# Stationary operands of 128 columns in the value projection and the score matmuls of a gated cross-attention kernel

## The chip, the cores and the metric

The kernel runs on one core of one Trainium2 chip. The metric is the device time of one execution in microseconds; the median of three runs of the kernel before is 411.07 us (410.23 to 413.1).

## The reference, cut to what matters

A block of gated cross-attention is followed by a gated mixture of experts. There are 8 sequences of 56 tokens with 256 features, and each has a context of 1500 rows with 256 features. Only the attention is touched by the change.

```python
q = _qdq(x) @ _qdq(wq).T + bq                       # (8, 56, 256), int8 fake quantisation
kv = cond @ wkv.T + bkv                             # cond: (8, 1500, 256)
k, v = jnp.split(kv, 2, axis=-1)                    # 16 heads of 16 features each
attn = jax.nn.softmax(jnp.einsum('bnhd,bmhd->bhnm', q, k) * scale, axis=-1)
o = jnp.einsum('bhnm,bmhd->bnhd', attn, v).reshape(B, N, C)
out = _qdq(o) @ _qdq(wp).T + bp
```

After it come the residual, a layer norm, the choice of two of 16 experts for every token, the experts (silu gates, at most 128 tokens each) and the sum.

## The kernel before, in words

The program is one block with one instruction stream for each engine, written out by hand, and semaphores between them. Three parts follow each other in time: the first projections of sequence 0 with the quantisation of the queries, then 64 attention slots, then the output projection and the experts.

A slot `u` is one pair of heads of one sequence: `b, i = divmod(u, 8)`. In slot `u` TensorE runs (function `pe_slot`)

- `scores(u)`: three matmuls of 500 context rows each. The stationary operand is the pair's part of `QC`, 112 columns (2 heads x 56 tokens) by 96 rows; the moving operand is the stacked keys `KS`. VectorE takes the row maxima from them (line 794).
- a projection for the next sequence (`project`, line 1035 through the helper `split3`). K0 to K5 are the keys: two feature halves by three chunks of 500 context rows, 6 matmuls with 500 moving columns, the stationary operand being 128 columns of the weights `wkvT`. V0 to V5 are the values: two tiles of 125 context rows each, 12 matmuls with 256 moving columns (the weights), the stationary operand being 125 columns of the context `cT`. Each value is a sum of three half-precision products (`SPLIT`), hence six matmuls for a tile.
- `turn_maxima(u - 1)`: one small matmul (line 1088) that turns the maxima into two rows of a PSUM bank. Its stationary operand is two columns wide and goes to the last quarter of the array's columns (`tile_position=(0, QR)`).
- a second projection or the attention outputs of two pairs (line 1112), in turn.
- `turned_scores(u - 1)`: 12 matmuls with 112 moving columns that compute the scores once more, turned, with the maxima subtracted (line 1101). Their stationary operand is `KS`, 128 columns since long, ScalarE takes the exponential of the result (line 501).

Which projection stands in which slot is a table:

```python
order = ("K0", "K1"), ("K2",), ("K3", "V0"), ("K4",), ("K5", "V1"), ("V2",), ("V3", "V4"), ("V5",)
```

The first name of a slot runs right behind `scores`, the second right behind `turn_maxima`. So V2, V3 and V5 follow the score matmuls, and V0, V1 and V4 follow the small matmul of line 1088. This holds for the 7 sequences 1 to 7; sequence 0 is projected before the slots, in an order of its own.

The context of a sequence is loaded in three chunks of 500 rows. ScalarE makes the upper halves (line 479), and the lower halves come from VectorE for sequences 0 and 1 (line 715) and from GpSimd from sequence 2 on (line 395). `need_lo(pe, n, c)` lets TensorE wait for chunk `c` of sequence `n`. `cT` and `QC` hold two sequences each.

GpSimd makes `QC` in two halves for each sequence (function `queries`, line 419, semaphore `qc_done`); `scores` waits for half 0 in slot `i = 0` and for half 1 in slot `i = 4`. At its start GpSimd fills constants (line 365 and those behind it); TensorE and VectorE wait until the count `EARLY` of them is reached.

Of the kernel before, what the change touches and what calls it, by code (L numbers as in the profile page):

```python
# [41 lines left out]
EPS = 1e-5  # L42
EARLY = 16
NCONST = 24
NSMALL = 3 * 16
# [64 lines left out]
def program(nc, x, ctx, cols, rows, gate, wq, wkv, wp, W13, W2, out):  # L110
    stack = ExitStack()
    with stack:
        def sb(name, shape, dt=F32):
            return stack.enter_context(nc.sbuf_tensor(name, shape, dt))
# [48 lines left out]
        q16 = sb("q16", [QR, NPAIR, T], F16)  # L163
        QC = sb("QC", [128, 2, QW], F16)
        par16 = sb("par16", [128, 2], F16)
        wkvT = sb("wkvT", [128, 2, NH, 2 * D], F16)

        c_in = sb("c_in", [128, NH, M])
        cT = sb("cT", [128, 2, 2, NH, M], F16)

# [87 lines left out]
        def need(eng, name, n):  # L258

            if n > 0:  # L260
                eng.wait_ge(s[name], n)
# [100 lines left out]
        def _(gp):  # L362
            c = Steps(gp, s["consts"])
            for t, v in ((mhalf, -0.5), (unmagic, -MAGIC), (ident, 0.0), (ident16, 0.0), (ones, 1.0), (ones16, 1.0), (before16, 1.0), (hm2, 1.0)):
                c.did(gp.memset(t[:], v))
# [662 lines left out]
        def _(pe):  # L1028
# [30 lines left out]
            def project_values(n, v):  # L1059
                bank = take(("V", n, v))  # L1060
                need_lo(pe, n, v // 2)
                for k in range(2):
                    t = 2 * v + k
                    last = split3(PS[0:KP, bank, k * D:(k + 1) * D], lambda a, h: cT[:, n % 2, a, h, t * KP:(t + 1) * KP],
                                  lambda a, h: wkvT[:, a, h, D:2 * D])
                last.then_inc(s["v_ready"], 1)

            def scores(u):
                b, i = divmod(u, NPAIR)
                need(pe, "aug_done", min(u - 1, SLOTS - NPAIR))  # L1070
                if i % 4 == 0:
                    need(pe, "qc_done", 2 * b + i // 4 + 1)
                for c in range(CH):
                    if i % 4 == 0:
                        pe.wait_ge(stacked[i // 4][c], 48 * (b + 1))
                    if c < 2:
                        need(pe, "red_done", 2 * (u - 1) + c + 1)
                    mm(PS[0:TP, c, 0:CW], QC[0:QR, b % 2, i * TP:(i + 1) * TP], KS[0:QR, b % 2, i, c * CW:(c + 1) * CW],  # L1078
                       start=True, stop=True).then_inc(s["sc_ready"], 1)
# [357 lines left out]
```

## Time and profile before

| | us |
|---|---|
| median of the three runs | 411.07 |
| lowest and highest run | 410.23, 413.1 |
| span of the profiled execution, first to last instruction | 405.0 |
| median less the span (what lies around it) | 6.07 |
| TensorE matmuls busy in the span | 358.6 |
| TensorE weight loads busy in the span | 269.3 |
| VectorE busy | 303.5 |
| ScalarE busy | 250.9 |
| GpSimd busy | 124.1 |

The profile is one execution. Times are read from the start of the span. PE is TensorE's matmul side and PEld its weight loads, which lie beside matmuls; the end of a matmul in the profile is modelled, so from one matmul to the next the starts are to be compared, not the ends. A row such as "64.23 1.47 ... x12" says that 12 instructions of one kind began at 64.23 us and that 1.47 us lie between the first start and the last end. DVE is VectorE, ACT ScalarE, POOL GpSimd, SP the queue that issues most transfers.

### The profile page before, as it was taken

Reading aid. Unit: us, or ns where it says so; the run is one execution under the profiler, and the core shown is the slowest. Engines: PE = TensorE matmul, PEld = TensorE weight load, DVE = VectorE, ACT = ScalarE, POOL = GpSimd, SP = SyncE. Lnnn points to the kernel's source line nnn. Section 1 sums busy time; section 2 is a strip of 40 time slices with the busy share of each in tenths; the row PEclk is TensorE's granted clock in tenths of the full one; section 3 lists DMA queues with packets and bytes.
Section 4 is the critical chain, followed back from the end, with each engine's and each line's share of the span. In section 5 each row is a group of like instructions: output and inputs, shape, how many; then the busy total and the mean of one; then the engine's idle time right before and its main releaser. Section 6 shows DMA issues by size and latency. Waiting matters only on the chain.

```text
span 405.0 us, 14019 instructions
## 1 busy us (share of the span) xinstructions
PE 358.6 (89%) x5793; PEld 269.3 (67%) x5793; DVE 303.5 (75%) x656; ACT 250.9 (62%) x412; POOL 124.1 (31%) x116
## 2 busy tenths in 40 slices
PE   0896899999998998998999999998864699999993
PEld 0663468668677766855866776786643587888882
DVE  3888886775776676586577668668896877999993
ACT  3476477777686676776768666567721535666761
POOL 6151462132022122222203300001101054787870
PEclk9999699999999999999999999999985858999998
DMA  7869965565294186166336208544000009635001
GB/s 253 196 157 197 241 146 134 87 159 136 58 171 115 53 152 182 54 106 175 103 61 125 54 14 142 129 137 141 3 2 2 1 1 306 191 116 163 2 0 45
DMA packets 34512, 45.65 MB, mean 113 GB/s; under 512 B 3995, under 2 KB 30299, under 8 KB 34323
## 3 DMA queue, kind: packets, MB, share of 16 engines
q1 hardware_dynamic: 33395, 43.74, 44.5%
q0 software_dynamic: 640, 0.78, 0.9%
q8 instruction: 46, 0.75, 0.8%
q10 hardware_dynamic: 416, 0.26, 0.3%
q14 instruction: 15, 0.12, 0.1%
HBM read 25.08 MB, written 0.47 MB: 63 GB/s over the span
## 4 chain that ended last, share of the span: by engine, by line
PE 76%; DVE 13%; issue 5%; ACT 2%; POOL 2%; DMA 1%; DVEq 0%; ACTq 0%; POOLq 0%
PE PS L1035 35%; PE PS L1101 9%; PE PS L1078 8%; PE PS L1112 7%; PE PS L1363 4%; PE PS L1322 3%; DVE mx L794 2%; PE PS L1088 2%; PE PS L1346 2%; PE PS L1312 1%; DMA x_in<-x 1%; DVE KN L743 1%; PE PS L1279 1%; DVE st L697 1%; DVE mtop L798 1%
## 5 line engine op out<-in xcount | busy, mean ns | idle before, releaser
L794 DVE TENSOR_REDUCE mx<-PS 112x1 f32<-112x500 f32 (+1 forms) x128 | 114.3, 933 | 52.8 <-PE PS L1078 52.7
L501 ACT ACTIVATE PT_all<-PS 128x1344 f32<-128x1344 f32 x64 | 82.6, 1290 | 10.1 <-PE PS L1101 9.9
L1035 PE MATMUL PS<-cT,wkvT 128*128 128x500 f16 x288 | 71.5, 385 | 18.0 <-POOL slot_of L404 11.2
L1035 PE MATMUL PS<-wkvT,cT 128*125 128x256 f16 x576 | 73.2, 279 | 0.0
L1035 PEld LDWEIGHTS PS<-wkvT,cT 128*125 128x125 f16 x576 | 65.3, 139 | 5.3 <-issue 0.5
L395 POOL TENSOR_TENSOR cT<-c_in,cT 128x1000 f16<-128x1000 f32 x18 | 37.5, 2082 | 86.9 <-ACT cT L479 86.9
L1035 PEld LDWEIGHTS PS<-cT,wkvT 128*128 128x128 f16 x288 | 27.5, 99 | 50.8 <-POOL slot_of L404 11.2
L486 ACT ACTIVATE KN<-PS,col_in 128x500 f16<-128x500 f32 x48 | 32.5, 677 | 40.6 <-PE PS L1035 40.6
L1078 PE MATMUL PS<-arena,QC 96*112 96x500 f16 x192 | 52.4, 380 | 3.1 <-issue 2.8
L1101 PE MATMUL PS<-QC,arena 98*128 98x112 f16 x768 | 49.2, 214 | 3.0 <-ACT QC L521 2.9
L493 ACT ACTIVATE V<-PS 125x512 f32<-125x512 f32 x48 | 28.7, 598 | 30.6 <-PE PS L1035 30.6
L1101 PEld LDWEIGHTS PS<-QC,arena 98*128 98x128 f16 x768 | 41.6, 99 | 8.3 <-ACT QC L521 3.1
L743 DVE SCALAR_TENSOR_TENSOR KN<-PS,col_in,KN 128x500 f16<-128x500 f32 x48 | 35.2, 736 | 12.8 <-ACT KN L486 12.0
L1112 PE MATMUL PS<-PT_all,V 125*17 125x56 f32 x2592 | 37.8, 213 | 0.1
L449 POOL TENSOR_TENSOR arena<-arena 88x512 f16<-88x512 f32 x17 | 24.8, 1458 | 31.2 <-ACT arena L527 31.1
L1035 PE MATMUL PS<-arena 88*128 88x256 f16 (+2 forms) x216 | 33.3, 306 | 0.8 <-ACT arena L635 0.7
L1112 PEld LDWEIGHTS PS<-PT_all,V 125*17 125x17 f32 x2592 | 33.3, 98 | 0.2 <-issue 0.2
L419 POOL TENSOR_TENSOR QC<-q,par 96x448 f16<-96x448 f16 x16 | 15.0, 943 | 57.1 <-PE PS L1101 55.3
L1035 PEld LDWEIGHTS PS<-arena 88*128 88x128 f16 (+2 forms) x216 | 22.5, 106 | 9.0 <-issue 1.2
L1078 PEld LDWEIGHTS PS<-arena,QC 96*112 96x112 f16 x192 | 20.3, 132 | 9.8 <-issue 3.8
L479 ACT ACTIVATE cT<-c_in 128x1000 f16<-128x1000 f32 x24 | 24.9, 1036 | 2.0 <-DMA c_in<-ctx 1.6
L1088 PEld LDWEIGHTS PS<-ident,nm 112*2 112x2 f16 x64 | 5.1, 79 | 21.9 <-issue 17.3
(207 smaller groups left out, 463.8 us busy)
## 6 DMA issues: line engine op xcount, KB each, us to landing
arena<-KN SPq DMA_DIRECT2D x144, 125.0 KB, 3.6
c_in<-ctx SPq DMA_DIRECT2D x24, 500.0 KB, 4.5
cT<-W SPq DMA_DIRECT2D x11, 352.0 KB
c_in<-W SPq DMA_DIRECT2D x6, 352.0 KB
cT<-W SPq DMA_DIRECT2D x11, 176.0 KB
arena<-place_far SPq DMA_DIRECT2D x1, 1568.0 KB, 10.0
c_in<-W SPq DMA_DIRECT2D x6, 176.0 KB
PT_all<-L_xattn_wkv SPq DMA_DIRECT2D x1, 512.0 KB, 6.1
```

The costliest lines, as they stand in the source:

```text
L395: gp.tensor_tensor(cT[:, n % 2, 1, :, c * CW:(c + 1) * CW], c_in[:, :, c * CW:(c + 1) * CW], cT[:, n % 2, 0, :, c * CW:(c + 1) * CW], ALU. ...
L449: gp.tensor_tensor(w2T[j % 2][:, 1], w2_s, w2T[j % 2][:, 0], ALU.subtract).then_inc(s["w2l_done"], 1)
L479: act.activation(cT[:, n % 2, 0, :, c * CW:(c + 1) * CW], c_in[:, :, c * CW:(c + 1) * CW], ACT.Copy).then_inc(s["th_done"], 1)
L486: act.activation(KN[:, oh, c, 0, :], PS[:, BANK["K", n, u], 0:CW], ACT.Identity, bias=bk_c[:, oh:oh + 1]).then_inc(s["kh_done"], 1)
L493: act.activation(V[:, n % 2, 2 * v:2 * v + 2, :, 0:DH], PS[0:KP, BANK["V", n, v], :].rearrange("p (t h j) -> p t h j", t=2, h=H), ACT.Copy ...
L501: act.activation(PT_all[:, u % 4, :].rearrange("p (c k) -> p c k", c=CH), PS[:, 3:6, 0:4 * TP], ACT.Exp, scale=SCORE).then_inc(s["exp_done ...
L743: dve.scalar_tensor_tensor(KN[:, oh, c, 1, :], PS[:, BANK["K", n, u], 0:CW], bk_c[:, oh:oh + 1], KN[:, oh, c, 0, :], ALU.add, ALU.subtract ...
L794: dve.tensor_reduce(mx[:, u % 2, k:k + 1], PS[0:TP, k:1 + k * (CH - 1), 0:CW], AX.XY, ALU.max).then_inc(s["red_done"], 1)
L1035: ins = mm(out_, w(a, h), x_(b, h), start=first and k == 0, stop=last and k == len(todo) - 1)
L1078: mm(PS[0:TP, c, 0:CW], QC[0:QR, b % 2, i * TP:(i + 1) * TP], KS[0:QR, b % 2, i, c * CW:(c + 1) * CW], start=True, stop=True).then_inc(s[" ...
L1101: last = mm(PS[:, 3 + t // 4, (t % 4) * TP:(t % 4 + 1) * TP], KS[0:QR + 2, b % 2, i, t * KP:t * KP + 128], QC[0:QR + 2, b % 2, i * TP:(i + ...
L1112: last = mm(PS[32 * j:32 * j + VW, bank, 0:S], V[:, b % 2, t, 4 * hg + j, :], PT[:, (2 * g + j // 2) % 4, t * TP + (j % 2) * S:t * TP + (j ...
```

## The change

The value projection's stationary operand gets 128 columns of `cT` instead of 125: the further three are the first rows of the next tile. They give three further rows of the result, which nobody reads. The context's last tile reads columns 1500 to 1503, so `cT` gets 1504 columns, and GpSimd fills the last four with zeros at its start. Where a tile now reaches into the next chunk (V1 and V3), the wait is for that chunk; in sequence 0 those two tiles (t = 3 and 7) stay at 125 columns. The score matmuls get 128 columns of `QC` instead of 112: the further 16 belong to the next pair, or for the last pair to 16 columns behind the end, which are filled with zeros. The wait for the second half of `QC` therefore moves from slot `i = 4` to slot `i = 3`. The two fills are counted among GpSimd's constants.

```diff
-EARLY = 16
-NCONST = 24
+EARLY = 18
+NCONST = 26
...
-        QC = sb("QC", [128, 2, QW], F16)
+        QC = sb("QC", [128, 2, QW + 128 - TP], F16)
...
-        cT = sb("cT", [128, 2, 2, NH, M], F16)
+        cT = sb("cT", [128, 2, 2, NH, KW], F16)
...
             c = Steps(gp, s["consts"])
+            c.did(gp.memset(cT[:, :, :, :, M:KW], 0.0))
+            c.did(gp.memset(QC[:, :, QW:], 0.0))
...
             def project_values(n, v):
                 bank = take(("V", n, v))
-                need_lo(pe, n, v // 2)
+                over = n > 0 and v % 2 == 1 and v < 5
+                need_lo(pe, n, v // 2 + over)
                 for k in range(2):
                     t = 2 * v + k
-                    last = split3(PS[0:KP, bank, k * D:(k + 1) * D], lambda a, h: cT[:, n % 2, a, h, t * KP:(t + 1) * KP],
+                    w = KP if n == 0 and t in (3, 7) else 128
+                    last = split3(PS[0:w, bank, k * D:(k + 1) * D], lambda a, h: cT[:, n % 2, a, h, t * KP:t * KP + w],
                                   lambda a, h: wkvT[:, a, h, D:2 * D])
...
-                if i % 4 == 0:
-                    need(pe, "qc_done", 2 * b + i // 4 + 1)
+                if i in (0, 3):
+                    need(pe, "qc_done", 2 * b + (i + 1) // 4 + 1)
...
-                    mm(PS[0:TP, c, 0:CW], QC[0:QR, b % 2, i * TP:(i + 1) * TP], KS[0:QR, b % 2, i, c * CW:(c + 1) * CW],
+                    mm(PS[:, c, 0:CW], QC[0:QR, b % 2, i * TP:i * TP + 128], KS[0:QR, b % 2, i, c * CW:(c + 1) * CW],
```

The order of TensorE's matmuls stays as it was. What moves is one wait. On TensorE, sequence 0, these are the score matmuls of slots 3 and 4 before the change, with what each waits for:

```order
L1078 MATMUL PS<-arena,QC 112x500 [waits red_done,aug_done]
L1078 MATMUL PS<-arena,QC 112x500 [waits red_done]
...
L1078 MATMUL PS<-arena,QC 112x500 [waits stacked1_0,red_done,qc_done,aug_done]
L1078 MATMUL PS<-arena,QC 112x500 [waits red_done,stacked1_1]
```

and the same place with the change:

```order
L1082 MATMUL PS<-arena,QC 128x500 [waits red_done,qc_done,aug_done]
L1082 MATMUL PS<-arena,QC 128x500 [waits red_done]
...
L1082 MATMUL PS<-arena,QC 128x500 [waits red_done,stacked1_0,aug_done]
L1082 MATMUL PS<-arena,QC 128x500 [waits red_done,stacked1_1]
```

The wait for the second half of the queries stands one slot earlier; `arena` is the memory of the stacked keys.

## Rows read from the trace of the kernel before

**Rows 1.** The page: busy time of the engines, and the chain that ended last

```profile
PE 358.6 (89%) x5793; PEld 269.3 (67%) x5793; DVE 303.5 (75%) x656; ACT 250.9 (62%) x412; POOL 124.1 (31%) x116
PE 76%; DVE 13%; issue 5%; ACT 2%; POOL 2%; DMA 1%; DVEq 0%; ACTq 0%; POOLq 0%
```

**Rows 2.** Busy time of each engine in stretches: the steady slots, and around 44 us

```profile
core 0: us, PE busy (x) PEld busy (x) DVE busy (x) ACT busy (x) POOL busy (x), PEclk, DMA share, GB/s
56.00:272.00 216.00, 209.97 (x4043) 156.13 (x4043) 149.16 (x308) 150.07 (x225) 45.92 (x29) 1.00 0.51 113
...
40.80:48.00 7.20, 6.20 (x26) 2.94 (x27) 5.29 (x9) 3.27 (x4) 2.11 (x4) 0.53 1.09 254
```

**Rows 3.** Groups of instructions, shapes apart: projections and scores, matmuls and weight loads

```profile
L1035 PE MATMUL PS<-wkvT,cT 128*125 128x256 f16 x576 | 73.2, 279 | 0.0
L1035 PEld LDWEIGHTS PS<-wkvT,cT 128*125 128x125 f16 x576 | 65.3, 139 | 5.3 <-issue 0.5
L1035 PEld LDWEIGHTS PS<-cT,wkvT 128*128 128x128 f16 x288 | 27.5, 99 | 50.8 <-POOL slot_of L404 11.2 <-issue 7.6 <-DVE cT L715 2.8
L1078 PEld LDWEIGHTS PS<-arena,QC 96*112 96x112 f16 x192 | 20.3, 132 | 9.8 <-issue 3.8 <-DVE mx L794 0.5 <-ACT sp_row L558 0.4
```

**Rows 4.** Timeline of TensorE's matmuls, value slots: V3 and V4 between scores

```profile
63.59 0.80 PE L1078 MATMUL PS<-arena,QC 96*112 96x500 f16 x3
64.23 1.47 PE L1035 MATMUL PS<-wkvT,cT 128*125 128x256 f16 x12
65.64 0.21 PE L1088 MATMUL PS<-ident,nm 112*2 112x112 f16 x1
65.78 1.52 PE L1035 MATMUL PS<-wkvT,cT 128*125 128x256 f16 x12
67.14 0.76 PE L1101 MATMUL PS<-QC,arena 98*128 98x112 f16 x12
67.73 0.80 PE L1078 MATMUL PS<-arena,QC 96*112 96x500 f16 x3
```

**Rows 5.** The same stretch on the side of the weight loads

```profile
64.02 1.44 PEld L1035 LDWEIGHTS PS<-wkvT,cT 128*125 128x125 f16 x12
...
65.77 1.28 PEld L1035 LDWEIGHTS PS<-wkvT,cT 128*125 128x125 f16 x12
...
67.68 0.39 PEld L1078 LDWEIGHTS PS<-arena,QC 96*112 96x112 f16 x3
```

**Rows 6.** Timeline of TensorE's matmuls, a key slot: K0 and K1 around line 1088

```profile
105.26 1.43 PE L1035 MATMUL PS<-cT,wkvT 128*128 128x500 f16 x6
106.62 0.21 PE L1088 MATMUL PS<-ident,nm 112*2 112x112 f16 x1
106.76 1.44 PE L1035 MATMUL PS<-cT,wkvT 128*128 128x500 f16 x6
```

**Rows 7.** Timeline of TensorE's matmuls, two places where scores start after a wait

```profile
255.20 0.84 PE L1078 MATMUL PS<-arena,QC 96*112 96x500 f16 x3 [0.66 <-issue]
...
274.38 0.84 PE L1078 MATMUL PS<-arena,QC 96*112 96x500 f16 x3 [0.22 <-ACT sp_row L558]
```

**Rows 8.** Timeline of all engines at the start: GpSimd's fills and TensorE's first matmul

```profile
0.84 0.10 POOL L365 MEMSET unmagic<- 112x1 f32 x1
...
7.16 1.04 POOL L390 TENSOR_TENSOR rstd<-var,mhalf 112x4 f32<-112x4 f32 x1 [1.84 <-DVE var L703]
...
11.20 2.66 PE L1035 MATMUL PS<-cT,wkvT 128*128 128x500 f16 x6 [11.20 <-POOL slot_of L404]
```

**Rows 9.** Timeline of GpSimd, the second half of QC for sequences 0 and 1

```profile
29.59 0.92 POOL L419 TENSOR_TENSOR QC<-q,par 96x448 f16<-96x448 f16 x1 [0.97 <-DMA q<-PT_all]
...
51.10 1.82 POOL L419 TENSOR_TENSOR QC<-q,par 96x448 f16<-96x448 f16 x2
```

**Rows 10.** Timeline of TensorE's matmuls around 44 us

```profile
40.84 2.50 PE L1035 MATMUL PS<-cT,wkvT 128*128 128x500 f16 x6 [2.35 <-DVE cT L715]
...
45.56 1.46 PE L1078 MATMUL PS<-arena,QC 96*112 96x500 f16 x3
```

## The prediction

> **What bounds the kernel now.** I read four views, from the coarse to the fine. The page's engines and its chain come first [rows 1]: TensorE's matmuls are busy for 358.6 us of 405.0, and 76% of the chain that ended last is TensorE. The reader is to see that a nanosecond taken from TensorE is likely to be a nanosecond of the whole, but that busy time alone does not say which of its instructions cost anything, since the weight loads (PEld, 269.3 us) lie beside the matmuls. Then the table by stretches [rows 2]: from 56 to 272 us, the steady slots, matmuls are busy for 209.97 of 216.00 us at a granted clock of 1.00, which is the level of 2.4 GHz. All other engines are under 151 us there. So in the slots TensorE goes from one matmul to the next without a pause, and what matters is the distance from start to start. Then the groups with shapes apart [rows 3]: a weight load of 125 columns is recorded at 139 ns, one of 112 columns at 132 ns, and one of 128 columns at 99 ns, although it loads more. That is the difference the change reaches for: 576 loads of the first kind and 192 of the second become loads of the third. Last the timeline of two value slots [rows 4, 5] and of a key slot [rows 6], which tell whether a load is waited for at all.
>
> **What a weight load costs where it lies.** In the stretch of V3, which follows the score matmuls, the first load begins at 64.02 us [rows 5] and the first matmul that uses it at 64.23 [rows 4]: the load lies beside the last score matmul. The twelve matmuls take 1.47 us to the end of the last, whose recorded length is about 0.28 [rows 3], so the distance is (1.47 - 0.28) / 11 = 0.108 us. The keys, whose loads are all of the short kind, give the rate of the array itself. Three scores start 64.23 - 63.59 = 0.64 us ahead of the next run, 0.21 each, and 0.80 - 2 x 0.21 = 0.38 us is the recorded length of a matmul of 500 columns [rows 4]. So six keys lie (1.43 - 0.38) / 5 = 0.21 us apart for 500 moving columns [rows 6], which is 0.1075 us for 256. The values thus run at the rate of their moving columns already; a load of 125 columns hides behind every matmul of 256. I price the loads inside a run of values at nothing. Their cover is the matmul before, 0.108 us long, and it stays.
>
> The load of the first score matmul has a shorter cover. It begins at 67.68 us [rows 5], and the matmul at 67.73 [rows 4]; before it stand the matmuls of line 1101, at a distance of (0.76 - 0.21) / 11 = 0.05 us. 67.14 + 12 x 0.05 = 67.74, so the scores start right on time: nothing to gain there either. The second and third score load lie behind 0.21 us each.
>
> What is left are the loads with no cover. The small matmul of line 1088 uses a quarter of the array's columns of its own, and the next load begins only behind it: at 65.77 us, when its matmul begins at 65.78 [rows 4, 5]. The run of values behind it takes 1.52 us instead of 1.47, so 0.05 us are paid for the bare load of 125 columns. The keys tell what is paid for a bare load of 128: K1 behind line 1088 takes 1.44 us, K0 behind the scores 1.43, so 0.01 us [rows 6]. The change saves 0.04 us at each such place.
>
> **The Trainium skill on this.** The groups show the 128-column load shorter than the 125-column one, 99 against 139 ns [rows 3]. The Trainium skill, page "TensorE: Matmul & The Clock Gate", section "Weight-path perf modes — Fast Weight Load (FWL) and DoubleRow", says why: the fast load comes on by itself where the stationary operand has 128 columns and is not single precision, and it was measured about twice as fast. The trace agrees in kind, with 99 against 139 ns recorded. The same page, section "Back-to-back issue gap", says that in a stream of loads and matmuls the distance is set by both together; that rule speaks for more than I forecast, and it is the second rival below. By it the sum would be some 29 us, by the rows on the starts it is about 1.
>
> **The sum.** V0, V1 and V4 of seven sequences follow line 1088: 3 x 7 = 21 places x 0.04 = 0.84 us. Two score groups start after a wait and are 0.84 us long instead of 0.80 [rows 7]: 2 x 0.03 = 0.06 us at best. The values of sequence 0 run ahead of the slots between other work; I give them nothing. The remaining edits:
> - Two more fills on GpSimd ahead of its constants. The nearest rows are its fills of 0.10 us [rows 8]; a strided one may take twice that, so 0.2 to 0.4 us. GpSimd then waits 1.84 us for VectorE before the power at 7.16 us, and TensorE's first matmul is at 11.20 [rows 8]; the wait hides both fills. Without that cover they would cost 0.4 us at most.
> - The wait for the second half of `QC` one slot earlier, in slot 3. Behind it on TensorE stand the scores and the whole slot, for which VectorE and ScalarE wait. For sequence 0 that half is done at 29.59 + 0.92 = 30.5 us [rows 9]; the scores of slot 2 start at 45.56 [rows 10], those of slot 3 behind them. For sequence 1 it is done at 51.10 + 1.82 = 52.9 us [rows 9], and its slot 3 comes eight slots later than that of sequence 0. Price: nothing.
> - The wait of V1 and V3 for the next chunk. K1 and K2 of the same sequence, two to six slots earlier on the same engine, already waited for chunks 1 and 2. Nothing.
> - Three or sixteen further rows of results: the matmul's time goes by its moving columns; the keys write 128 rows at the same rate as the scores write 112 [rows 4, 6]. Nothing.
>
> Bounds of the whole: at the bare places from 0 to the full 0.05 us (0 to 1.05); inside the runs (0.108 - 0.1075) x 555 is 0.3 us at best, and as much lost if rounding goes the other way. So -1.4 to +0.3 us. I take 0.84 + 0.06 = 0.9, from the row of K1. All of it lies on the path, since TensorE runs without a pause there. The profiled execution then goes from a span of 405.0 to 404.1; 6.07 us lie around the span to the median of 411.07, and I count them as unchanged: 410.2 us. The three runs lie between 410.23 and 413.1, so a median may differ by about 1 us of itself.
>
> **Rivals.**
> 1. The first load stays bare at its old price, because the short load needs something that tiles at odd offsets of 125 columns do not have, or the 0.04 us come back as a longer wait. For it: the short loads in the trace are of `wkvT` and the stacked keys, none of `cT` or `QC`. Against it: the stacked keys are read at offsets of 125 columns too and load in 99 ns on line 1101. Time: 411.1 us.
> 2. The recorded load time is all on the path: 576 x (139 - 99) = 23.0 us and 192 x (132 - 99) = 6.3 us, 29.4 us in all [rows 3], so 411.07 - 29.4 = 381.7 us. For it: PEld is busy for two thirds of the span. Against it: 139 ns of load do not fit one behind the other into a distance of 108 ns, so they overlap. The Trainium skill's rule on the distance, named above, is this rival's.
> 3. Slower: TensorE's clock falls once more. At 40.8 to 48.0 us the granted clock is 0.53, the level of 1.2 GHz for nearly all of it, behind a wait of 2.35 us for VectorE [rows 2, 10], and six key matmuls take 2.50 us instead of 1.43. The price of one such stretch is 6.20 x (1 - 0.53) = 2.9 us of busy time. If TensorE, done sooner, waits longer in the pauses of the slots and the clock falls there too, the time is 410.2 + 2.9 = 413.1 us. It decides from one more such fall on, as one costs three times the gain. Against it: the clock is 1.00 over all of 56 to 272 us, pauses included, and 0.04 us make no pause.
>
> **How the numbers follow.** Forecast 80%: 410.2 us, of itself 409.3 to 411.5. Rival 1 9%: 411.1. Rival 2 4%: 381.7. Rival 3 7%: 413.1. The range from 408.8 to 412.6 holds the forecast with its bounds, the spread of medians and rival 1; it leaves out rivals 2 and 3, and with a little of the forecast's own tail that is under 2 in 10. A change of 1% (4.1 us) is about what a measurement of this kernel can tell from none. Faster by more than that is rival 2 and little else: 5%. Slower by more needs rival 3 with a second fall: 3%. Within 1%: 92%.
>
> **What would show it.** In the profile after, the value and score loads should read about 99 ns in the groups and PEld's busy time should fall by some 29 us, while matmuls keep their distance of 0.108 and 0.21 us. The run of values behind line 1088 should take 1.48 us instead of 1.52, the one behind the scores still 1.47. The slots from 56 to 272 us should shorten by some 0.8 us. I am wrong if a run of values behind the scores gets shorter as well, if scores start sooner than 0.05 us behind line 1101, if a pause that is not there now stands in front of slot 3, or if the granted clock falls below 1.00 in the slots.

## The result and the profile after

The changed kernel takes 407.63 us (median, 404.54 to 409.92), the kernel before, run beside it, 410.15 us (406.56 to 413.78). The ratio is 0.9947, with a 95% interval of 0.9923 to 0.9971: 0.5% faster, some 2.2 us. The ratios in this document leave out executions more than 1.5% above the fastest of the same kernel, while the times are medians of all, among them single executions of 523.54 us (before_later_sum), 604.38 us (after_shift128) and 1925.24 us (after_shift64_later_sum). The forecast of 410.2 us meant 0.9 us less than before, and its range ended at 408.8. So the direction and a change within 1% came as forecast, the time fell out of the range, and more than half of the gain came from somewhere else. Of the 2.6 us between forecast and result, 0.9 are the base: I counted from 411.07, the median of three runs; the median of twenty is 410.15.

The profiled execution of the changed kernel has a span of 406.1 us and took 407.8 us. Its page, with the engines, the queue that carries instructions, and the chain:

```profile
PE 357.6 (88%) x5793; PEld 255.5 (63%) x5793; DVE 304.8 (75%) x656; ACT 250.8 (62%) x412; POOL 124.8 (31%) x118
...
q8 instruction: 47, 0.77, 0.9%
...
PE 78%; DVE 13%; issue 4%; ACT 2%; DMA 1%; POOL 1%; DVEq 0%; ACTq 0%; POOLq 0%
```

Weight loads are busy for 13.8 us less than in [rows 1], TensorE's matmuls for 1.0 us less. The span is 1.1 us longer than that of before, though the kernel is faster: single executions of either kernel scatter by some 3 us either way, and the profiled one of before was among its quickest (two more executions, below, have spans of 409.6 and 409.9). That also corrects the table ahead: 1.7 us lie around the span, not 6.07.

Groups with shapes apart, weight loads (busy, mean ns of one, idle before):

```profile
L1037 PEld LDWEIGHTS PS<-wkvT,cT 128*128 128x128 f16 x564 | 54.2, 99 | 14.2 <-issue 1.7
...
L1037 PEld LDWEIGHTS PS<-cT,wkvT 128*128 128x128 f16 x288 | 27.7, 99 | 54.4 <-issue 12.2 <-POOL zero L404 11.2 <-DVE cT L717 2.9
L1082 PEld LDWEIGHTS PS<-arena,QC 96*128 96x128 f16 x192 | 15.6, 98 | 10.0 <-issue 1.7 <-DVE mx L796 0.6 <-ACT sp_row L560 0.4
```

Lines have moved by two to four: 1035 is now 1037, 1078 is 1082, 1088 is 1092, 1101 is 1105, 1112 is 1116. Against [rows 3] the loads of the values went from 139 to 99 ns, those of the scores from 132 to 98. The change does what it says.

The timeline of TensorE's matmuls in the slot of V3 and V4:

```profile
66.82 0.80 PE L1082 MATMUL PS<-arena,QC 96*128 96x500 f16 x3
67.46 1.47 PE L1037 MATMUL PS<-wkvT,cT 128*128 128x256 f16 x12
68.86 0.21 PE L1092 MATMUL PS<-ident,nm 112*2 112x112 f16 x1
69.00 1.48 PE L1037 MATMUL PS<-wkvT,cT 128*128 128x256 f16 x12
70.33 0.76 PE L1105 MATMUL PS<-QC,arena 98*128 98x112 f16 x12
70.92 0.80 PE L1082 MATMUL PS<-arena,QC 96*128 96x500 f16 x3
```

The reader sees the forecast come true to the hundredth: the values behind the scores take 1.47 us as before, those behind line 1092 take 1.48 instead of 1.52 [rows 4], scores start 0.59 us behind the start of line 1105's run as they did. Score start to score start, the slot takes 4.10 us instead of 4.14.

**Where the other gain is.** I cut both executions at the starts of the score groups. From slot 6 to 12, six slots, the kernel before takes 24.05 us and the changed one 23.97, and each of the next sequences repeats that (24.04 and 23.97 from slot 14 to 20, 22 to 28, 30 to 36). But the slots left out between them (12 and 13, 20 and 21, 28 and 29, 36 and 37, 44 and 45, 51 to 53) differ by more: 59.36 us in all before, 57.77 after. One of them in the kernel before, slot 36, on TensorE's timeline:

```profile
185.47 1.39 PE L1112 MATMUL PS<-PT_all,V 125*17 125x56 f32 x96
186.79 0.76 PE L1101 MATMUL PS<-QC,arena 98*128 98x112 f16 x12
187.39 0.80 PE L1078 MATMUL PS<-arena,QC 96*112 96x500 f16 x3
189.83 1.44 PE L1035 MATMUL PS<-cT,wkvT 128*128 128x500 f16 x6 [1.63 <-POOL cT L395]
```

and the same slot of the changed kernel:

```profile
188.48 1.39 PE L1116 MATMUL PS<-PT_all,V 125*17 125x56 f32 x96
189.80 0.77 PE L1105 MATMUL PS<-QC,arena 98*128 98x112 f16 x12
190.40 0.80 PE L1082 MATMUL PS<-arena,QC 96*128 96x500 f16 x3
191.04 0.58 PE L1037 MATMUL PS<-cT,wkvT 128*128 128x500 f16 x2
192.20 1.00 PE L1037 MATMUL PS<-cT,wkvT 128*128 128x500 f16 x4 [0.58 <-issue]
```

TensorE stands still in both. Before, it does so for 1.63 us between the scores and the keys; the profile names GpSimd's write of `cT`, though the same chunk had been waited for slots earlier. After, it is for 0.58 us, in the middle of six matmuls of one accumulation, where no wait can stand; the profile says "issue". Such a pause stands once in every sequence, and in the trace of before its places are exactly 618 matmuls apart (behind matmul 953, 1571, 2189, 2807, 3425; the sixth, behind 4044, is 619 on), after the change mostly 619.

What comes every 618 matmuls? In the changed kernel TensorE has 5793 matmuls, as many loads and, counted in the trace, 434 instructions that only wait: 12,020. One of two queues that carry instructions (q8 in the page above) moved 0.77 MB in 47 packets, 16 KB each; 12,020 / 47 is 255.7, so 256 instructions a packet. And in the kernel before, 618 matmuls with their loads and 44 waits are 1,280 instructions, five packets. So I read it as follows: TensorE's instructions come in blocks of 256, and at the end of one in five it stands still until the next has come. That block's last instructions lie behind the 96 small matmuls of the attention outputs (line 1112), which with their loads use up 192 instructions in 1.39 us, three quarters of a block; the rest of such a slot, 22 matmuls, takes some 2.7 us, 16 instructions per us. In slots 12 to 44 of every trace without a shift the packet's transfer starts 2.2 to 2.9 us before TensorE goes on, however long the pause. The counts say the same for all runs: the traces but that of after_shift128 hold 86 pauses over 0.25 us in slots 6 to 54, and in each the number of TensorE's instructions (matmuls, loads and waits) ahead of the pause leaves 192 or 193 when divided by 256. None lies more than 28 matmuls behind the outputs; four lie among them.

A sequence is 620 matmuls, 1,284 instructions with its 44 waits: four more than five blocks, so the pause moves two matmuls towards the outputs in each sequence. The kernel before has 442 waits, the changed one 434, one less in a sequence. In the traces a load holds one wait itself and a wait instruction one or two more. In slots 3 and 4 the first score matmuls had two and four waits (the order shown with the change), which took one and two wait instructions; now they have three each, which take one and one. So its pauses come 618 or 619 matmuls apart and stand elsewhere: in the six sequences 0, 1, 2, 2, 3 and 3 matmuls further behind the outputs than before. At 0.21 us a matmul, these 11 would give the next block 2.3 us more in all, an estimate that holds if the transfers start at the same places. That was my theory after the first traces; the experiments had to separate it from the loads.

### The profile page after: what moved, and what is told of

Read it like the earlier page. It is cut to its first block, busy times and chain, and to the rows that moved or that the text cites. A ratio compares the mean times of both kernels' runs of the same rounds, so it can differ in the third digit from the quotient of the medians.

```text
span 406.1 us, 14013 instructions
## 1 busy us (share of the span) xinstructions
PE 357.6 (88%) x5793; PEld 255.5 (63%) x5793; DVE 304.8 (75%) x656; ACT 250.8 (62%) x412; POOL 124.8 (31%) x118
## 4 chain that ended last, share of the span: by engine, by line
PE 78%; DVE 13%; issue 4%; ACT 2%; DMA 1%; POOL 1%; DVEq 0%; ACTq 0%; POOLq 0%
PE PS L1037 37%; PE PS L1105 10%; PE PS L1082 8%; PE PS L1116 8%; PE PS L1367 4%; PE PS L1326 3%; PE PS L1092 2%; DVE mx L796 2%; PE PS L1350 2%; DVE mtop L800 2%; PE PS L1316 1%; DMA x_in<-x 1%; PE PS L1283 1%; DVE st L699 1%; DVE KN L745 1%
## 5 line engine op out<-in xcount | busy, mean ns | idle before, releaser
L1037 PE MATMUL PS<-cT,wkvT 128*128 128x500 f16 x288 | 72.7, 389 | 21.3 <-POOL zero L404 11.2
L1037 PE MATMUL PS<-wkvT,cT 128*128 128x256 f16 (+1 forms) x576 | 72.4, 277 | 0.0
L1037 PEld LDWEIGHTS PS<-wkvT,cT 128*128 128x128 f16 (+1 forms) x576 | 55.5, 100 | 14.2 <-issue 1.7
L1082 PE MATMUL PS<-arena,QC 96*128 96x500 f16 x192 | 51.4, 374 | 1.6 <-issue 1.4
L481 ACT ACTIVATE cT<-c_in 128x1000 f16<-128x1000 f32 x24 | 24.9, 1035 | 1.5 <-DMA c_in<-ctx 1.0
L1082 PEld LDWEIGHTS PS<-arena,QC 96*128 96x128 f16 x192 | 15.6, 98 | 10.0 <-issue 1.7
```

The costliest lines, as they stand in the source:

```text
L481: act.activation(cT[:, n % 2, 0, :, c * CW:(c + 1) * CW], c_in[:, :, c * CW:(c + 1) * CW], ACT.Copy).then_inc(s["th_done"], 1)
L1037: ins = mm(out_, w(a, h), x_(b, h), start=first and k == 0, stop=last and k == len(todo) - 1)
L1082: mm(PS[:, c, 0:CW], QC[0:QR, b % 2, i * TP:i * TP + 128], KS[0:QR, b % 2, i, c * CW:(c + 1) * CW], start=True, stop=True).then_inc(s["sc_ ...
```

## The experiments

The ratios are to the kernel before on the same chip, with 95% intervals. "Slots 6 to 54" is the distance of two score groups in the profiled execution, which leaves out the scattered start and the end; "pauses" is the sum over the six stretches named above, which is 52.26 us where no pause stands in them (52.04 with the short loads).

| run | time, us | ratio | slots 6 to 54 | pauses |
|---|---|---|---|---|
| kernel before | 410.15 | 1 | 199.71 | 59.36 |
| before_look1 | 411.71 | one execution | 200.69 | 60.35 |
| before_look2 | 412.10 | one execution | 200.27 | 59.93 |
| changed kernel | 407.63 | 0.9947 (0.9923 to 0.9971) | 197.66 | 57.77 |
| again | 407.11 | 0.9936 (0.9901 to 0.9971) | 197.31 | 57.43 |
| values_only | 408.25 | 0.9976 (0.9939 to 1.0014) | 197.30 | 57.42 |
| scores_only | 407.61 | 0.9977 (0.9939 to 1.0015) | 198.81 | 58.46 |
| layout_only | 409.36 | 1.0004 (0.9969 to 1.0039) | 199.24 | 58.90 |
| before_later_sum | 409.4 | 1.0009 (0.9971 to 1.0046) | 201.07 | 60.55 |
| after_later_sum | 406.49 | 0.9921 (0.9885 to 0.9958) | 196.24 | 56.17 |
| before_one_wait | 408.99 | 0.9919 (0.9877 to 0.9961) | 199.45 | 59.12 |
| after_repeat_wait | 410.6 | 1.002 (0.999 to 1.005) | 201.66 | 61.78 |
| after_shift64 | 408.69 | 0.9896 (0.9854 to 0.9937) | 197.78 | 52.04 |
| after_shift64_again | 408.51 | 0.9955 (0.9925 to 0.9985) | 198.47 | 52.04 |
| after_shift128 | 408.91 | 0.9958 (0.9926 to 0.9990) | not read | not read |
| after_shift32 | 424.89 | 1.0243 (1.0167 to 1.0319) | 215.82 | 59.67 |
| after_shift64_later_sum | 407.01 | 0.9869 (0.9811 to 0.9927) | 198.17 | 52.04 |
| before_shift64 | 402.09 | 0.9793 (0.9746 to 0.9839) | 194.37 | 52.26 |
| before_shift64_again | 403.02 | 0.9798 (0.9749 to 0.9847) | 198.06 | 52.27 |
| loads_at_64 | 401.74 | 0.9746 (0.9698 to 0.9794) | 193.61 | 52.04 |

The slots of after_shift128 are not read because its profiled execution, the one of 604.38 us, has a granted clock of 0.55 from 60 us on.

**One part of the change alone.** Values alone and scores alone each leave the other's stationary operand at its old width; the third has the buffers, the fills and the moved wait, with no short load at all; the fourth is the changed kernel once more.

```diff
 values_only:
-                    mm(PS[:, c, 0:CW], QC[0:QR, b % 2, i * TP:i * TP + 128], KS[0:QR, b % 2, i, c * CW:(c + 1) * CW],
+                    mm(PS[0:TP, c, 0:CW], QC[0:QR, b % 2, i * TP:(i + 1) * TP], KS[0:QR, b % 2, i, c * CW:(c + 1) * CW],
 scores_only:
-                    w = KP if n == 0 and t in (3, 7) else 128
+                    w = KP
 layout_only: both
```

> Value tiles of 128 columns, score matmuls back at 112; the wider buffers, the two fills and the moved wait stay. Theory A (only loads that nothing hides count, 21 places of 0.04 us): 0.84 us under the kernel before, ratio about 0.998, and the run of twelve values behind line 1092 at 1.48 us. Theory B (the values save more than the bare loads, in a place that the steady slots do not show): 1.5 to 2.2 us under it, ratio 0.9945 to 0.9965. Theory C (the further gain does not come from loads at all but from when instruction fetches or GpSimd's work meet TensorE's and VectorE's): about as theory A, and the profile's pauses in the slots with K5 differ from those of the kernel before by more than 0.8 us in sum, either way.

> Score matmuls of 128 columns, value tiles back at 125; the rest as in the changed kernel. Theory A: no difference, at most 0.1 us, ratio 1.000; the distance of scores stays 0.215 us. Theory B for the scores: the ratio is that of the whole change, 0.9947, or half of what it saves beyond 0.9 us, 0.6 to 1.3 us, ratio 0.997 to 0.9985. Theory C: anything within 1 us, from pauses alone.

> All loads as in the kernel before (125 and 112 columns); only the wider buffers, the two fills at GpSimd's start and the moved wait of the changed kernel. Theory A: ratio 1.000 within its interval. Theory C in the form that the moved wait or the fills shift instruction fetches or GpSimd's work: 1.0 to 1.5 us under the kernel before, ratio 0.9965 to 0.9975.

> The changed kernel once more. If the first ratio of 0.9947 was in part chance, this one lies nearer to 0.998 (theory A); if it is real, it lies within 0.9925 and 0.997 again. The steady slots 2, 4 and 6 are 0.04 us shorter than in the kernel before in both profiles in either case.

The steady slots obey the loads and nothing else: 23.97 us for six of them with short value loads (values_only, again), 24.04 without (scores_only, layout_only). The times don't separate as cleanly: each part alone has an interval that reaches from 0.994 to 1.0015, and the ratio of layout_only is no different from 1 (its median is 409.36 us, that of the kernel before beside it 410.77). The changed kernel repeats. With these four alone I would have said that the two loads give 1 us each, but the slots show 0.03 us in one place for the scores. Something that moves by itself takes part.

**The start.** Between slots 2 and 5 the profiled execution of the changed kernel loses 5 us to before's: 19.27 against 14.07 us. On its VectorE:

```profile
49.87 5.66 DVE L800 TENSOR_TENSOR mtop<-mx 112x1 f32<-112x1 f32 x1
55.57 0.16 DVE L803 TENSOR_SCALAR nm<-mtop 112x1 f16<-112x1 f32 x1
```

An operation on one column that takes 0.16 us elsewhere is recorded at 5.66, while GpSimd works without a gap:

```profile
46.59 0.62 POOL L436 TENSOR_TENSOR row_in<-row_in,tg 112x256 f32<-112x256 f32 x1
47.30 2.37 POOL L438 TENSOR_TENSOR x<-x_in,row_in 112x1024 f32<-112x1024 f32 x1
49.63 1.81 POOL L421 TENSOR_TENSOR QC<-q,par 96x448 f16<-96x448 f16 x2
51.41 4.11 POOL L397 TENSOR_TENSOR cT<-c_in,cT 128x1000 f16<-128x1000 f32 x2
```

Was that a cost of the change, which would hide a still larger gain? I took two more executions of the kernel before, and both kernels with GpSimd's sum of the residual (the two rows at 46.59 and 47.30) moved behind its last queries:

```diff
-            gp.tensor_tensor(bp_r, bp_r, tg[:, 0:1].to_broadcast([TP, D]), ALU.mult).then_inc(s["xb_ready"], 1)
...
-            gp.tensor_tensor(x1[:], x_in[:], bp_r.unsqueeze(1).to_broadcast([TP, TT, D]), ALU.add).then_inc(s["xb_ready"], 1)
...
+            for t in range(TT):
+                last = gp.tensor_tensor(x1[:, t], x_in[:, t], bp_r, ALU.add)
```

> The kernel before, unchanged, for a second profile of it. Its profiled execution took 405.0 us of span, while most executions of it lie near 408.4. Theory D (VectorE stands behind GpSimd's long run of additions at about 48 to 55 us, for a time that differs from execution to execution, and this makes the difference beyond 0.9 us): slots 2 to 5 take 18 to 20 us here, not the 14.1 us of the first profile. Theory E (the pauses for instruction fetches in the slots with K5 make it): those pauses sum to 6.4 us or more, against 5.1 to 5.4 in the two profiles of the changed kernel. Both may hold.

> The same, for a third profile. Theories D and E as for the second one. If both profiles have slots 2 to 5 at 18 to 20 us, as the changed kernel has, theory D does not tell the two kernels apart.

> The kernel before with GpSimd's two additions for the residual (3.0 us at 48 us) moved behind its last queries, and cut in four. Theory D: VectorE's longest stand shrinks, 1.5 to 4 us under the kernel before, and the scatter of the runs gets smaller. Theories A and E: within 0.5 us of the kernel before.

> The same move in the changed kernel. Theory D: with the additions away in both, the change is worth 0.9 us (theory A's bare loads) between these two kernels. Theory E, or theory B (loads that matter elsewhere): still 2 to 3 us between these two. In either case this is the fastest of the kernels so far if theory D holds at all.

Both further executions of the kernel before show 19.3 and 19.4 us from slot 2 to 5. The loss comes and goes in both kernels and tells nothing of the change. Moving the sum is worth nothing before (1.0009); after, its interval (0.9885 to 0.9958) overlaps that of the changed kernel itself. The theory that the start makes the difference finds no support.

These executions gave something else, the price of a pause that lasts long. TensorE's timeline in slot 36 of before_look1, and its stretch by windows (busy time of each engine, then granted clock):

```profile
189.97 0.80 PE L1078 MATMUL PS<-arena,QC 96*112 96x500 f16 x3
192.96 2.68 PE L1035 MATMUL PS<-cT,wkvT 128*128 128x500 f16 x6 [2.18 <-POOL cT L395]
```

```profile
core 0: us, PE busy (x) PEld busy (x) DVE busy (x) ACT busy (x) POOL busy (x), PEclk, DMA share, GB/s
...
192.50:196.00 3.50, 3.04 (x9) 1.07 (x10) 0.22 (x2) 0.32 (x1) 0.00 (x0) 0.52 0.52 156
```

Behind a pause of 2.18 us the granted clock is 0.52, the level of 1.2 GHz, and six keys take 2.68 us instead of 1.43. From the first key to the first of the values TensorE takes 2.79 us instead of 1.51, so it loses 1.3 us to it. This is the fall of the clock of my third rival, but it was there before the change. It stands in slot 36 of before_look1, before_later_sum, after_repeat_wait and before_one_wait, and in neither trace of the changed kernel, whose pause there is 0.58 us in the rows above.

**One wait more, one wait less.** The changed kernel with the old wait stated again in slot 4 has as many instructions as before; the kernel before with one wait for both halves of `QC` in slot 0 has as few as the changed one, at old loads and buffers.

```diff
 after_repeat_wait:
+                if i == 4:
+                    need(pe, "qc_done", 2 * b + 2)
 before_one_wait:
-                if i % 4 == 0:
-                    need(pe, "qc_done", 2 * b + i // 4 + 1)
+                if i == 0:
+                    need(pe, "qc_done", 2 * b + 2)
```

> The changed kernel with the wait for the second half of QC stated again in slot 4, where it costs nothing by itself; it gives TensorE back the one wait instruction per sequence that the change took away (442 instead of 434). Theory E1 (TensorE's instructions come in blocks of 256, a pause stands wherever a block's end falls behind the outputs' burst, and one instruction less per sequence moves those ends): the pauses stand at every 618th matmul again instead of every 619th, they sum to about 6.9 us as in the kernel before instead of 4.1 to 5.7, and the ratio goes from 0.9940 to about 0.997. Theory B (the loads themselves save the rest): pauses and ratio as in the changed kernel, 0.994.

> The kernel before, all its loads and buffers, with one wait for both halves of QC in slot 0 of each sequence instead of one in slot 0 and one in slot 4: one wait instruction less per sequence, as in the changed kernel. Theory E1: the pauses stand at every 619th matmul, and this alone is worth 0.5 to 1.5 us, ratio 0.9965 to 0.999. Theory B: ratio 1.000, pauses of 6.7 to 7.5 us in sum.

A wait that was satisfied long ago takes the whole gain away: 410.6 us, 1.002, with the steady slots still at their 23.97. Its pauses stand at the same matmuls as in the kernel before, 618 apart; in this one trace they sum to 61.78 - 52.04 = 9.7 us, more than the 6.9 that I expected, with one fall of the clock. And one wait less gives the kernel before a ratio of 0.9919 without a short load; this rests on the seven of its twelve executions up to 409.02 us, and the median of all twelve, 408.99 against 410.63 us beside it, is only 0.4% less. Its profiled execution has the pauses at the places of the changed kernel, and one fall of the clock in slot 36, which hides most of the gain in the table's columns. But layout_only, too, has one wait less and old loads, and its ratio of 1.0004 does not agree with 0.9919. In the traces its pauses sum to 58.90 - 52.26 = 6.6 us, those of scores_only, with old value loads, to 6.2 and those of before_one_wait to 6.9, against 7.1, 8.1 and 7.7 in the three of the kernel before and 5.7 and 5.4 in the two of the changed kernel. So one wait less is enough for about half of what the pauses gave back; why they are shorter still where the short loads come with it is not shown. Instructions that do nothing decide over about as much time as the change.

**The block ends moved on purpose.** Waits on a semaphore that already holds, at the very start of TensorE's program, where it waits for 11 us anyhow, shift every later block end: 64, 128 or 32 instructions (two waits each). With 64 and 32 the first matmul stays at 11.2 to 11.6 us; with 128 it starts at 17.98 us in the one trace, so that run moves more than block ends.

```diff
-            pe.wait_ge(s["consts"], EARLY)
+            for k in range(128):
+                pe.wait_ge(s["consts"], EARLY)
```

> The changed kernel with 64 more wait instructions (128 waits on a count that is long reached) at TensorE's start, where it has nothing to do for 7 us. All later ends of instruction blocks fall 64 instructions earlier in the program. Theory E1: the pauses move to other places and their sum changes by more than 1 us, either way, and the time with it. Theory B: nothing changes, ratio 0.994.

> The same with 128 more wait instructions at the start. Theory E1: as for 64, at other places again; the one of the two whose pauses are shorter in sum is the faster. If the waits take longer than the 7 us that TensorE has free, its first matmul starts after 11.2 us, and by so much the run is longer. Theory B: ratio 0.994.

> The kernel before with 128 waits that hold already put at TensorE's start, which are 64 instructions: no load and no buffer is changed, only the places at which TensorE's instruction blocks end move. Theory (most of the gain is pauses between blocks): the pauses of slots 12, 20, 28, 36, 44 and 51 go or move, the six stretches that hold them fall from 59.4 to about 53, and the whole comes to 406 to 408 us, a ratio of 0.990 to 0.995, with the steady slots still at 24.04 us. Rival (the short loads are the gain): the ratio is 1.00 and the stretches stay at 59 to 60 us.

> The changed kernel with the same 64 instructions ahead, once more, on the same chip as the kernel before with them. Theory: steady slots 23.97 us, the six stretches near 52 us, and some 0.8 us less than the kernel before with the 64 instructions, the price of the bare loads at equal block ends. Rival (the loads are worth the whole 2.2 us or more): 2 us less than the kernel before with the 64 instructions.

> The changed kernel with 32 instructions ahead in place of 64. Theory: the pauses move by 32 instructions, so that they stand at other places of the slots than in the changed kernel and than with 64; the time follows the sum of the pauses in the profile, between 0.988 and 1.002, and the steady slots stay at 23.97 us. Rival: block ends have no part in it, and the ratio is that of the changed kernel, 0.994 to 0.995.

> The changed kernel with the 64 instructions ahead and with GpSimd's sum of the residual moved behind its last queries. If the two edits add up, the ratio is 0.985 to 0.988 (404.5 to 406 us); if the sum's place is worth nothing, as in the kernel before, it equals the run with the 64 instructions alone, 0.990.

This shows the cause beyond the loads. The kernel before, its loads and buffers untouched, goes to 402.09 us (0.9793), a larger gain than any version of the change without a shift and more than the 406 to 408 us that I expected; 5.3 to 6.3 us of it lie in slots 6 to 54 (194.37 us against 199.71 to 200.69). The changed kernel goes to 424.89 us with 32 instructions, out of the range that I expected: slower than before by 2.4% as the ratio has it (three of six executions) and by 3.4% by the medians (410.85 beside it). With 128 it takes 408.91 us (0.9958). With 32, block ends fall into the short matmuls right behind the outputs. Slot 11 of after_shift32:

```profile
86.46 1.39 PE L1117 MATMUL PS<-PT_all,V 125*17 125x56 f32 x96
87.78 0.52 PE L1106 MATMUL PS<-QC,arena 98*128 98x112 f16 x7
91.72 0.41 PE L1106 MATMUL PS<-QC,arena 98*128 98x112 f16 x5 [3.42 <-issue]
```

TensorE pauses 3.42 us after seven of twelve matmuls, the granted clock behind it is 0.71 from 91.7 to 95 us, and such a pause stands in every sequence: slots 6 to 54 take 215.82 us. With 64 the block end lies, by count, among the outputs themselves (32 matmuls before 953, and the outputs are 837 to 932), and the pauses in slots 12, 20, 28, 36, 44 and 51 are gone: 52.04 us for their stretches. But with 64 another block end comes to stand behind the outputs of slots 9, 17, 25 and 33. There TensorE pauses at some and not at others. Slot 34 of after_shift64_again:

```profile
178.31 1.39 PE L1117 MATMUL PS<-PT_all,V 125*17 125x56 f32 x96
179.63 0.76 PE L1106 MATMUL PS<-QC,arena 98*128 98x112 f16 x12
180.23 0.80 PE L1083 MATMUL PS<-arena,QC 96*128 96x500 f16 x3
183.68 1.44 PE L1037 MATMUL PS<-cT,wkvT 128*128 128x500 f16 x6 [2.64 <-issue]
```

and of before_shift64:

```profile
180.59 0.76 PE L1102 MATMUL PS<-QC,arena 98*128 98x112 f16 x12
181.20 0.80 PE L1079 MATMUL PS<-arena,QC 96*112 96x500 f16 x3
181.83 1.43 PE L1035 MATMUL PS<-cT,wkvT 128*128 128x500 f16 x6
```

Both kernels have the same 64 instructions ahead; they differ in the loads and in one wait per sequence, and the changed one is 6.4 us slower than the kernel before. My expectation of 0.8 us less was wrong: I had taken 64 instructions to mean equal block ends, and they were not. The sum's move on top of the 64 (0.9869, interval to 0.9927, four executions) is not told apart from the first run of the 64 alone (0.9896), though it lies below the second (0.9955); its median of 407.01 us is 1.5 to 1.7 us below theirs, and the expected 404.5 to 406 us did not come.

**The loads alone, at equal block ends.** What was missing was a pair with the same number of instructions on TensorE and the same shift: the kernel before with 64 once more, and the changed kernel with 64 and with the wait of slot 4 stated again.

```diff
+            for k in range(128):
+                pe.wait_ge(s["consts"], EARLY)
...
+                if i == 4:
+                    need(pe, "qc_done", 2 * b + 2)
```

> The kernel before with the 64 instructions ahead, once more, as the partner of the next run on the same chip. Theory: 402 to 403 us, ratio 0.977 to 0.984, one long pause of some 1.8 us in slot 10 and none in slots 12, 20, 28, 36, 44 and 51. Rival (the first look at it was a lucky one): 0.99 or above.

> The changed kernel with the wait of slot 4 stated again, so that TensorE has as many instructions as the kernel before, and with the 64 instructions ahead: against the run beside it the loads of 128 columns are all that differs, and every block of instructions ends at the same matmul. Theory (the loads are worth 0.8 us, the rest of the gain was where pauses fell): steady slots 23.97 us where the partner has 24.04, no pause that the partner has not, and 0.5 to 1.2 us less than the partner, some 401.3 us, a ratio of 0.975 to 0.982: faster than both kernels. Rival (the loads are worth the whole 2.2 us): 400 us or less. Rival (the loads are worth nothing): the partner's time.

The pair of medians is 403.02 and 401.74 us, 1.3 us apart; with both runs of the kernel before with 64 against the one of loads_at_64 the means of the executions that the ratios keep differ by 1.7 us, with a standard error of 0.7, and those of all by 0.3. That excludes nothing between 0.3 and 3 us, so it holds the forecast's 0.9 and also the rival's 2.2. The traces are sharper. From slot 6 to 54 before_shift64 takes 194.37 us and loads_at_64 193.61; both have one pause, in slot 10, of 1.75 and 1.68 us by the starts, and no other over 0.25. The score matmuls of slots 6 and 54 with the pause of slot 10 between them, first in before_shift64, then in loads_at_64:

```profile
67.09 0.80 PE L1079 MATMUL PS<-arena,QC 96*112 96x500 f16 x3
...
86.36 0.60 PE L1035 MATMUL PS<-cT,wkvT 128*128 128x500 f16 x2 [1.59 <-issue]
...
261.46 0.80 PE L1079 MATMUL PS<-arena,QC 96*112 96x500 f16 x3
```

```profile
64.49 0.80 PE L1085 MATMUL PS<-arena,QC 96*128 96x500 f16 x3
...
83.64 0.59 PE L1037 MATMUL PS<-cT,wkvT 128*128 128x500 f16 x2 [1.52 <-issue]
...
258.10 0.80 PE L1085 MATMUL PS<-arena,QC 96*128 96x500 f16 x3
```

So 0.76 - 0.07 = 0.69 us are the loads'. Three places ahead of slot 6 and behind 54 add some 0.1 at the same 0.04. The page of loads_at_64:

```profile
PE 355.1 (89%) x5793; PEld 254.8 (64%) x5793; DVE 304.9 (76%) x656; ACT 250.6 (63%) x412; POOL 124.9 (31%) x118
...
PE 78%; DVE 12%; issue 4%; ACT 3%; DMA 1%; POOL 1%; DVEq 0%; ACTq 0%; POOLq 0%
```

It is the fastest of all, 0.9746 (0.9698 to 0.9794), and beats both kernels; some 2% of that are where blocks of instructions end (0.9793 and 0.9798 without a short load). The rest, 0.5%, is more than the loads' 0.2% by the traces, but the intervals overlap. Its partner's second profile holds one pause that the first had not, 2.1 us in slot 18 with a fall of the clock behind it, which is why its column reads 198.06.

## Why the prediction was right in its parts and wrong in the sum

- **Bare loads behind line 1088, 0.04 us each: right.** 1.52 became 1.48 us. Every stretch of six steady slots holds two such places and went from 24.04 to 23.97, the two slots between them hold one and take 8.02 instead of 8.06 where no pause stands. Over slots 6 to 54, with 18 of the 21 places, that is 0.46 us in the steady stretches (140.34 to 139.88) and 0.22 in the others (52.26 to 52.04); with the remaining three some 0.8, where 0.84 were forecast.
- **Loads inside runs, nothing: right.** The values behind the scores still take 1.47 us. The second rival, 29.4 us, is out. Its arithmetic shows a trap: 576 loads of 139 ns would be 80 us, but [rows 3] gives 65.3 us of busy time, since loads overlap one another too. For the same reason my sign that PEld's busy time should fall by some 29 us was wrong: it fell by 13.8 us [rows 1], and of that the slots got back 0.7 to 0.8. The loads fell by 40 ns and the distance stayed at 0.108 us. The rule of the Trainium skill that the rival leaned on, "TensorE: Matmul & The Clock Gate", section "Back-to-back issue gap", has loads and matmuls set the distance together, pipelined; the rival read it as a sum, and no such sum is seen here.
- **Scores, 0.06 us at best: right in size.** In their old place they start as soon as before, and one pair of slots at the end (58 to 59) went from 2.47 to 2.44 us.
- **Fills, chunk waits, further rows, nothing: right** as far as layout_only (1.0004) can show it; no new pause stands in front of V1, V3 or slot 3.
- **"Price: nothing" for the wait moved to slot 3: the step that failed.** I asked what is queued behind the wait and whether the data is there, and that part holds. What I didn't ask is how many instructions it is. Eight went away, the places where TensorE runs out of instructions moved, and with them pauses that summed to 59.36 - 52.26 = 7.1 us in the kernel before. In the traces of the changed kernel the same stretches hold 57.77 - 52.04 = 5.7 and 5.4 us, and the fall of the clock that one trace of the kernel before shows behind them is missing. That is the second part of the gain: the distance from slot 6 to 54 fell from 199.7, 200.7 and 200.3 us in three executions to 197.7 and 197.3, by 2.7 us, of which 0.7 are the loads' and 2.0 the pauses'. With the wait stated again the whole gain is gone (1.002). How much the moved wait is worth without the short loads is less sure: about half of the 2.0 us in the traces, and 1.0004 and 0.9919 in two runs that disagree.
- **"TensorE goes from one matmul to the next without a pause": wrong as a reading of [rows 2].** 209.97 of 216.00 us busy left 6.0 us of which I said nothing. A timeline of slot 36 that I had read before the prediction shows 1.63 us of them at 189.83 us, put down to GpSimd's write of `cT`, and I passed over it, though my third rival speaks of pauses in the slots.
- **Rival 3, a further fall of the clock: wrong way round.** It exists, behind pauses that the kernel before has already, and neither trace of the changed kernel shows it in the slots. That the change removed it is not shown: before_one_wait has as few instructions and has it.
- **The range** rested on 0.9 us, a scatter of 1 us and a base that was 0.9 us high. Had the pauses been seen, the step for a moved instruction stream would have had ends of several us on both sides: a shift of 32 made the changed kernel slower than before by 2.4%.

What stays open: why a pause at the same distance behind the outputs lasts 0.53 us in one execution and 1.49 in the next (slot 28 of before_look1 and before_later_sum), why with 64 instructions ahead the block end behind slots 9, 17, 25 and 33 costs much at some and nothing at others, and how much of the 2 us would be left over many executions. Transfers that the SP queue issues in the same slots may have a part in it; no run took them away. That blocks hold 256 instructions is worked out from counts, and that the pauses are waits for a block rests on those counts, on the starts of the packets and on the shifts, not on a record that says so.

## What to carry to other kernels

A weight load costs only where nothing lies beside it: look for the matmuls that start later than the array's own rate allows, and count those, not the busy time of the loads. Before pricing a change of any instruction stream, look at the slots in which the engine's busy time falls short with "issue" or an implausible releaser behind it, in the middle of an accumulation above all; if they repeat at a fixed count of instructions, adding or dropping a few instructions that do nothing can be worth more than the change, and a comparison that doesn't hold the count equal measures both. Where bursts of very small matmuls lie, try a few shifts and time each, and do it last, since any later edit of that engine's program moves the ends again.

## What the runs showed that I had not expected

- TensorE stands still for 0.2 to 3.4 us at the end of one in five blocks of its instructions, behind 96 matmuls that use up three quarters of a block in 1.39 us; eight instructions out of 12,028 move the time by up to 0.8%, 64 put ahead of the kernel before by 2%, and 32 make the changed kernel 3 to 4% slower than it is without them.
- Some pauses were followed by about 3 us at the level of 1.2 GHz (a granted clock of 0.52 behind 2.18 us in slot 36 of before_look1, a loss of 1.3 us); a longer one was not (2.64 us in slot 34 of after_shift64_again, where six keys behind it take 1.44 us).
- An operation of VectorE on one column was recorded at 5.66 us instead of 0.16 while GpSimd ran six computing instructions in a row. What holds it there was not tried.
